# Attention mixes issued block by block or two blocks at a time, in a two-layer attention and experts kernel

## The reference, cut to what matters

```python
Q = (input_Q @ W_Q.T + b_Q).reshape(batch, -1, 16, 64).transpose(0, 2, 1, 3)   # K, V likewise
scores = einsum('bhqd,bhkd->bhqk', Q, K) / sqrt(64)
scores = where(attn_mask[:, None, :, :], -10000.0, scores)
attn = softmax(scores, axis=-1)
out = einsum('bhqk,bhkd->bhqd', attn, V)          # "the mix" below
return out.transpose(0, 2, 1, 3).reshape(batch, -1, 1024) @ W_out.T + b_out
```

## Time and profile before

| | us |
|---|---|
| median of 3 runs | 285.18 |
| lowest, highest | 283.87, 287.22 |
| the profiled execution | 284.33 |
| its span, first to last instruction | 282.6 |
| around the span | 1.7 |
| mean granted clock of TensorE | 0.991 |

### The profile page before, as it was taken

The page is one execution under the profiler, slowest core; times in us unless marked ns, Lnnn a source line. Parts: engine busy times, 40 slices in busy tenths (PEclk is TensorE's granted clock), DMA queues, the critical chain, the costliest instruction groups (busy, mean ns, idle before and its releaser), DMA issues.

```text
span 282.6 us, 6748 instructions
## 1 busy us (share of the span) xinstructions
PE 257.6 (91%) x1929; PEld 203.9 (72%) x1929; DVE 218.3 (77%) x666; ACT 191.1 (68%) x456; POOL 183.0 (65%) x272
## 2 busy tenths in 40 slices
PE   7787999998778989989999999999899899879994
PEld 4455766676556768758877777788677579869993
DVE  3999889889959786799677777886887919775653
ACT  2398879887879686857866676786867434824542
POOL 7367999675698674845833555575356998944550
PEclk9999999999999999999999999999999999979998
DMA  6469375100033665644666757565620000000000
GB/s 199 179 181 284 122 262 144 46 0 3 1 74 78 140 141 117 146 95 98 167 185 151 195 117 196 145 180 154 150 58 0 2 0 1 2 0 5 19 0 21
DMA packets 21284, 28.66 MB, mean 101 GB/s; under 512 B 3456, under 2 KB 13440, under 8 KB 21120
## 3 DMA queue, kind: packets, MB, share of 16 engines
q1 hardware_dynamic: 20816, 28.01, 37.8%
q10 hardware_dynamic: 432, 0.22, 0.3%
HBM read 10.13 MB, written 3.41 MB: 48 GB/s over the span
## 4 chain that ended last, share of the span: by engine, by line
PE 63%; DVE 14%; issue 8%; POOL 5%; DMA 4%; ACT 3%; SPq 1%; ACTq 0%; DVEq 0%; POOLq 0%
PE bank L1169 15%; PE bank L1322 13%; PE bank L1174 5%; PE bank L1176 5%; PE bank L1175 5%; PE bank L1294 4%; PE bank L1295 4%; PE bank L1288 3%; POOL probs L560 2%; PE bank L1335 2%; DVE probsT L906 2%; DVE masked L890 2%; DMA shared<-in_w00T 1%; PE bank L1409 1%; DMA q<-q_split 1%
## 5 line engine op out<-in xcount | busy, mean ns | idle before, releaser
L560 POOL TENSOR_SCALAR probs<-probs,rsum 128x512 f32<-128x512 f32 x128 | 88.6, 699 | 69.2 <-DVE rsum L899 68.3
L705 ACT ACTIVATE probs<-masked,neg_max 128x512 f32<-128x512 f32 x128 | 91.8, 718 | 12.3 <-DVE neg_max L890 8.7
L1169 PE MATMUL bank<-ident,probs 128*128 128x128 f32 x512 | 78.5, 276 | 5.0 <-DVE probsT L906 3.5
L1169 PEld LDWEIGHTS bank<-ident,probs 128*128 128x128 f32 x512 | 58.4, 141 | 22.4 <-POOL probs L560 10.2
L890 DVE CUSTOM_DVE_ANT_0 masked<-bank,mask 128x512 f32<-128x512 f32 x64 | 43.7, 683 | 16.3 <-PE bank L1295 15.8
L713 ACT ACTIVATE probsT<-bank 128x512 f32<-128x512 f32 x74 | 43.5, 588 | 16.1 <-PE bank L1169 15.9
L1322 PE MATMUL bank<-probsT,val 128*32 128x256 f32 (+1 forms) x512 | 46.6, 384 | 0.7 <-ACT mixT L723 0.7
L906 DVE COPY probsT<-bank 128x512 f32<-128x512 f32 x54 | 36.7, 679 | 9.0 <-PE bank L1169 8.8
L890 DVE CUSTOM_DVE_ANT_0 masked<-bank,shared 128x512 f32<-128x512 f32 x64 | 43.2, 677 | 0.5 <-PE bank L1288 0.4
L1322 PEld LDWEIGHTS bank<-probsT,val 128*32 128x32 f32 (+1 forms) x512 | 24.7, 123 | 18.7 <-issue 5.3
L1288 PE MATMUL bank<-parts 128*128 128x512 f32 x64 | 31.1, 488 | 5.6 <-DVE neg_max L890 4.9
(11 more groups left out here) (253 smaller groups left out, 542.2 us busy)
## 6 DMA issues: line engine op xcount, KB each, us to landing
k_both<-k_low SPq DMA_DIRECT2D x32, 128.0 KB, 3.1
k_both<-k_high SPq DMA_DIRECT2D x32, 128.0 KB, 2.9
q<-q_split SPq DMA_DIRECT2D x32, 128.0 KB, 2.4
q<-q_split SPq DMA_DIRECT2D x32, 64.0 KB, 2.0
parts<-staged_k SPq DMA_DIRECT2D x7, 256.0 KB, 2.6
w_flat<-in_w SPq DMA_DIRECT2D x1, 1536.0 KB, 7.9
staged_k<-k_high SPq DMA_DIRECT2D x2, 512.0 KB, 3.2
staged_k<-k_low SPq DMA_DIRECT2D x2, 512.0 KB, 3.9
```

The lines of the kernel that those rows point to most:

```text
L560: pool.tensor_scalar(p, p, rsum[:, u % NCOL:u % NCOL + 1], 1.0, ALU.mult, ALU.mult).then_inc(normed, 1)
L705: act.activation(probs[:, u % NP, :], masked[:, u % NS, :], ACT.Exp, scale=-1.0, bias=neg_max[:, c:c + 1], accum_out=sums[:, c:c + 1]).the ...
L1169: ins = pe.transpose(dst[0:rows, t * P:t * P + P], src, ident[:, :])
```

## The change

The blocks 8 to 21 of layer 1 are paired (8 with 9, and so on to 20 with 21). The mixes of a pair are issued together in the odd block's step, the even block's into columns 0 to 255 of the mix bank and the odd one's into columns 256 to 511. Copies and projections of a pair are issued together too, in the odd block's steps. The semaphore `mixed` is counted once for a pair, so waits on it are rewritten (`mixes_done`, `slots_free`). Since turned probabilities of four blocks now live at a time, pairs use slots 0, 1 and slots 2, 3 of `probsT` in turn. Blocks 22 and 23 and layer 0 stay as they are.

```diff
--- before.py
+++ after.py
@@ -81,6 +81,9 @@
         self.mix_at = self.end + (1 if last else (2, 3)[layer])
         self.copy_at = self.mix_at + (2 if layer == 1 and not last else 1)
         self.out_at = self.copy_at + 1
+
+        self.paired = layer == 1 and m < 22
+        self.slot = 2 * ((m // 2 + 1) % 2) if layer else 0
 
 
 def make_blocks():
@@ -178,6 +181,25 @@
 def mixes(k):
 
     return k.b + 1 if k.layer == 0 else k.m - 5
+
+
+def mixes_done(m):
+
+    return m + 1 if m < 8 else (9 + (m - 8) // 2 if m < 22 else m - 6)
+
+
+def slots_free(k):
+
+    if k.layer == 0:
+        return k.m - 1 if k.m >= 2 else 0
+    return mixes_done(k.m - 4) if k.m >= 12 else mixes_done(6 + k.m % 2)
+
+
+def pair_of(k):
+
+    if not k.paired:
+        return [k]
+    return [BLOCKS[k.m - 1], k] if k.m % 2 else []
 
 
 def turns_of_stack0(m):
@@ -419,6 +441,11 @@
 
             return 0 if e < STEPS else (e + 1) % 2
 
+        def half_of(k):
+
+            c = SQ * (k.m % 2) if k.paired else 0
+            return slice(c, c + SQ)
+
         def jobs_done(groups):
 
             return 1 + max(n for j, n in NUMBER.items() if (j[0] in ("k", "q") and j[1] - 16 in groups)
@@ -709,18 +736,18 @@
                 k, h, qt = unit(u)
                 act.wait_ge(turned, u + 1)
                 if k.m >= 2:
-                    act.wait_ge(mixed, k.m - 1)
-                act.activation(probsT[:, k.m % 2, h, :, qt * P:qt * P + P],
+                    act.wait_ge(mixed, slots_free(k))
+                act.activation(probsT[:, k.m % 2, k.slot + h, :, qt * P:qt * P + P],
                                turn_bank[u % 2][:, :].rearrange("p (k q) -> p k q", q=P),
                                ACT.Copy).then_inc(copied[u % 2], 1)
 
             def mix_copy(k):
                 n = mixes(k)
-                act.wait_ge(mixed, k.m + 1)
+                act.wait_ge(mixed, mixes_done(k.m))
                 if n >= 3:
                     act.wait_ge(projected_out, n - 2)
                 bias = bv1[:, k.g:k.g + 1] if k.layer else bv0[:, 0:1]
-                act.activation(mixT[:, n % 2, :], mix_bank[:, 0:SQ], ACT.Identity, bias=bias).then_inc(mix_copied, 1)
+                act.activation(mixT[:, n % 2, :], mix_bank[:, half_of(k)], ACT.Identity, bias=bias).then_inc(mix_copied, 1)
 
             def job(j):
 
@@ -792,7 +819,8 @@
 
                 for k in BLOCKS:
                     if t == k.copy_at and (k.layer or k.g == 3):
-                        mix_copy(k)
+                        for one in pair_of(k):
+                            mix_copy(one)
                 for j in PLAN.get(t - 1, ()):
                     job(j)
                 if 0 <= t + LEAD - 2 < TOTAL:
@@ -902,8 +930,8 @@
                 k, h, qt = unit(u)
                 dve.wait_ge(turned, u + 1)
                 if k.m >= 2:
-                    dve.wait_ge(mixed, k.m - 1)
-                dve.tensor_copy(probsT[:, k.m % 2, h, :, qt * P:qt * P + P],
+                    dve.wait_ge(mixed, slots_free(k))
+                dve.tensor_copy(probsT[:, k.m % 2, k.slot + h, :, qt * P:qt * P + P],
                                 turn_bank[u % 2][:, :].rearrange("p (k q) -> p k q", q=P)).then_inc(copied[u % 2], 1)
 
             def job(j):
@@ -927,7 +955,7 @@
                     two, half = j[1:]
                     dve.wait_ge(job_done, n + 1)
                     if two >= 1:
-                        dve.wait_ge(mixed, 8 if two < NV1 else 8 + 2 * (two - NV1 + 1))
+                        dve.wait_ge(mixed, 8 if two < NV1 else mixes_done(9 + 2 * (two - NV1)))
                     dve.tensor_copy(val1[:, two % NV1, 2 * half:2 * half + 2, :],
                                     job_bank[:, :].rearrange("p (k c) -> p k c", k=2)).then_inc(free, 1)
                 elif name == "ln" and j[1] >= 2:
@@ -1315,13 +1343,14 @@
                     v = val1[:, two % NV1, :, odd * P:odd * P + P]
                     first = last = True
                 if first and k.m:
-                    pe.wait_ge(mix_copied, mixes(k) - 1)
+                    pe.wait_ge(mix_copied, mixes(pair_of(k)[0] if pair_of(k) else k) - 1)
                 w = k.width
                 for i in range(NK):
                     for h in range(k.heads):
-                        ins = pe.matmul(mix_bank[w * h:w * h + w, 0:SQ], v[:, i, w * h:w * h + w],
-                                        probsT[:, k.m % 2, h, i, :], start=(first and i == 0), stop=(last and i == NK - 1))
-                ins.then_inc(mixed, 1)
+                        ins = pe.matmul(mix_bank[w * h:w * h + w, half_of(k)], v[:, i, w * h:w * h + w],
+                                        probsT[:, k.m % 2, k.slot + h, i, :], start=(first and i == 0), stop=(last and i == NK - 1))
+                if k.m % 2 or not k.paired:
+                    ins.then_inc(mixed, 1)
 
             def project_out(k):
                 n = mixes(k)
@@ -1358,9 +1387,11 @@
                     job(j)
                 for k in BLOCKS:
                     if t == k.mix_at:
-                        mix(k)
+                        for one in pair_of(k):
+                            mix(one)
                     if t == k.out_at and (k.layer or k.g == 3):
-                        project_out(k)
+                        for one in pair_of(k):
+                            project_out(one)
                 if 0 <= t < TOTAL:
                     turn(t)
```

## The result

The changed kernel takes 287.14 us, the median of 20 runs (285.13 to 289.72); the kernel before, run beside it, 284.64 (283.09 to 287.22). The ratio is 1.0087, 95% interval 1.0060 to 1.0114: slower by 2.5 us, where -0.3 was forecast. The profiled execution took 286.08, its span 284.2, with a mean granted clock of TensorE of 0.992.

A forecast was written before the change was run, and what follows sets the result against it. The prediction took PE to bound the second layer's stage, busy 7.80 of 7.80 us. Its terms, -1.2 + 0.4 + 0.3 + 1.3 - 1.1, summed to -0.3 us: 284.9 us, range 283.0 to 287.6.

The forecast's parts named there:

- The saving of 0.30 us a pair: On PE, a second mix directly behind the first pays no entry or exit edges: 0.30 us saved, at most 2.1 over seven.
- Rival 4: In the double mix, the second mix pays its edges again, so nothing is saved: +0.9 to +1.5, 286.1 to 286.7; chance 8%.
- 0.1 a pair for late maxima: Steady stage: PE waits for DVE maxima that come late, 0 to 0.3 us a pair, taken as 0.1, +0.4 in all.
- rival 2: Steady stage: DVE becomes the bound, +2.8 over four pairs in place of +0.4, 287.3; chance 9%.
- First pair +0.3: Pair 8/9: two DVE waits, 1.35 us, go while block 9's step gets 1.73 more; taken as 0.3 us slower.
- Pair 18/19 +1.3: Router of batch 0: block 18's mix, hidden there, returns in the open, 1.73 less a 0.44 projection: 1.3 us slower.
- Steady stage, pairs 10/11 to 16/17: 4 x -0.30: Layer 1's four middle pairs, PE taken as busy throughout: each saves 0.30 us, -1.2 in all.
- Pair 20/21, -1.1: Last steps: block 20's mix leaves the path, -1.6, and later projections give back 0.5: 1.1 us faster.
- both blocks now stand ahead of the transposes ... about 0.5 later: Last steps, pair 20/21: both blocks' projections precede the transposes and end about 0.5 us later relative to DVE.
- The q stacks at zero: Stacked q of even blocks loses cover, left -0.2 to +0.2 us; costed at zero, up to 0.2 each in the range.
- Rival 1, the clock: Router of batch 0: TensorE's clock falls behind PE's longer idling, under the double mix: +1.4, so 286.3; chance 25%.
- Rival 3: Router of batch 0: nothing is given back, as DVE ends block 18's stretch sooner; saving whole, -2.1, 283.1; chance 8%.

The follow-up runs named there:

- experiment 3: Only pair 10/11 paired, with batch 1's turning of normalised rows one step later: 283.89 us, ratio 0.9968 against the kernel before.
- experiment 2: Changed kernel with one pair at a time, against the kernel before: 18/19 alone +1.32 us, 10/11 alone costs 1.1, 16/17 alone +0.5 in its stages.

## Why the prediction was wrong

- *The saving of 0.30 us a pair*: right. A single pair with nothing in its way gave 0.29 in its stages (experiment 3). Rival 4 is out: no edge in the middle.
- *0.1 a pair for late maxima*: right, 0.09 on PE's timeline; stages 13 and 15 gave -0.18 and -0.21 against -0.2. DVE did not become the bound there (rival 2 out). In stage 17, where it has the statistics too, PE did wait 0.62 for its copy, but the chain through POOL set the stage.
- *First pair +0.3*: +0.30. *Pair 18/19 +1.3*: +1.32, and +1.32 alone.
- ***The step that failed: "Steady stage, pairs 10/11 to 16/17: 4 x -0.30".*** Two of the four stages were not steady. I had read the earlier trace rows at one place and multiplied by four, and listed "the three places in the layer where PE is not the bound" from waits that exist; the ends of two layer-norm chains, DVE's statistics and POOL's rows, had less slack (0.85 us in stage 11, 0.76 in stage 17) than the pairing took, and a slack is no wait. Stage 11 came at +0.75 for -0.2, stage 17 at +0.95 for -0.2: 2.1 of the 2.4 us by which the sum of stages missed. The working that was missing is one subtraction per hand-over: the producer's end from the consumer's start, against 2.03 or 1.59, with 0.15 for the hand-over.
- *Pair 20/21, -1.1*: the place was right, the gain 0.3 too large. DVE's 1.96 is gone as forecast. Without 18/19 ahead the same pair gave -1.27, and the projection of block 18 (0.42 in experiment 2) is most of the 0.47 between them. So it was the term "both blocks now stand ahead of the transposes ... about 0.5 later" that was short: 1.59 less 0.80, it is 0.8, and the chain ends on a copy of ACT (0.34 at 225.41) in place of DVE's.
- *The q stacks at zero*: right; no scores waited for them.
- *Rival 1, the clock*: it came true in part. 12 of 26 executions of the changed kernel had a mean clock under 0.983, but of the three profiles with a new fall only one had its fall at the router, with 1.6 for the 1.4 I gave it; two had it at the first pair (1.7), which I hadn't named. I gave it 25% as if it came always or never; it comes in a share of the executions. It is part of why the median, 287.14, lies above the undisturbed profiled execution, 286.08.
- *Rival 3*: out; stage 19 gave nothing back, and PE waited 2.16 there for the 2.4 I had worked out.

The range held the time and "slower by more than 1%" was not reached, but the forecast of -0.3 was on the wrong side of +2.5 (1.7 to 3.2), and for the reason above, not for scatter. The range was wide enough only because it reached into rivals 1 and 2; neither is what carried the miss.

## What to carry to other kernels

Before moving independent work away from a stretch, look for every chain across engines that starts and ends in it, and subtract the producer's end from the consumer's start. That slack is in no list of waits, and what is taken out beyond it comes back as idle time. A saving measured in one repetition of a loop is multiplied only over the repetitions that carry no job of their own. Take the instances where it pays, and leave the others: here four pairs of seven, with one job a step later, took 0.5% off, and all seven added 0.9%. Where a wait is found, look for a second hand-over that would have been late by as much before mending the first.

## What the runs showed of the hardware

- Thirty-two records of the 64-column halves in a row keep one pace, 0.216 us a pair of records across two blocks' weights; only going in and out of that shape costs, 0.30 us together.
- Whether TensorE's clock falls behind a pair of waits differs between executions of one kernel: two waits of 0.76 to 0.78 us at 121 to 124 left it whole in the undisturbed profiles and in the third of the three taken later, and ended in 0.57 over the next 4 us in the first. Each such fall cost 1.6 to 1.7 us of its stage. With ten filling matmuls in the waits at the router the share of executions with a mean clock under 0.983 was 1 of 12 in place of 12 of 26.
- A hand-over from POOL to PE takes 0.14 to 0.15 us from the end of POOL's row to the start of PE's matmul (140.07 to 140.22 with pair 10/11 alone, 189.14 to 189.29 in the changed kernel).
